# Edge attention with four gather buffers, two PSUM banks and the carried sums first; the message stage's first layer in pairs of steps

## What is computed

```python
# layer 0, for every edge
h = silu(edge_attr_8 @ fc_w1 / sqrt(8))                 # 8 -> 64: the first layer
w = (h @ fc_w2 / 8).reshape(-1, 5, 64)                  # 64 -> 320: the weights of five paths
# the weights times the sender's scalars and vectors make the messages, summed over each receiver

# layer 1, for every edge
scores = einsum(q[dst], k[src] + ef @ We + be) * scale * ew
m  = segment_max(scores, dst);  ex = exp(scores - m[dst])
out = segment_sum(ex / segment_sum(ex, dst)[dst] * v[src], dst)
# then the output projection, layer norms and a feed-forward of 1024
```

## Time and profile before

| What | us |
|---|---|
| median of three runs | 2969.75 |
| the profiled execution's own time | 2986.19 |
| its span | 2984.5 |
| message stage (164 steps) | about 70 to 1196 |
| order, projections, table of steps | about 1196 to 1476 |
| attention stage (96 steps) | about 1476 to 2777 |
| output stage | about 2777 to 2984 |

### The profile page before, as it was taken

The page is one execution under the profiler, slowest core; times in us unless marked ns, Lnnn a source line. Parts: engine busy times, 40 slices in busy tenths (PEclk is TensorE's granted clock), DMA queues, the critical chain, the costliest instruction groups (busy, mean ns, idle before and its releaser), DMA issues. The chain is left out here.

```text
span 2984.5 us, 40835 instructions
## 1 busy us (share of the span) xinstructions
PE 2102.1 (70%) x9125; PEld 1572.3 (53%) x9126; DVE 2219.6 (74%) x3394; ACT 1531.1 (51%) x4900; POOL 1741.0 (58%) x1849
## 2 busy tenths in 40 slices
PE   1699999999999999499235444455444554445898
PEld 0577777777777777233123333333333333333677
DVE  5688888888888888455367777777777787777555
ACT  0677777777777777133133333333333333333566
POOL 4477777777777777222266666666666666665011
PEclk8799999999999999699667777777777777777899
DMA  3422222222222222589566666666666666665000
GB/s 119 144 81 81 81 82 82 82 80 82 82 82 82 80 82 81 101 252 253 181 177 168 175 175 168 170 169 170 179 169 170 170 169 179 169 169 163 7 14 14
DMA packets 157682, 382.65 MB, mean 128 GB/s; under 512 B 47682, under 2 KB 62402, under 8 KB 157410
## 3 DMA queue, kind: packets, MB, share of 16 engines
q0 software_dynamic: 101968, 313.67, 37.6%
q1 hardware_dynamic: 55426, 57.40, 7.2%
q10 hardware_dynamic: 272, 11.42, 1.1%
HBM read 356.98 MB, written 36.80 MB: 132 GB/s over the span
## 5 line engine op out<-in xcount | busy, mean ns | idle before, releaser
L1497 PE MATMUL ps_sum<-kv_e,ident 128*128 128x264 f32 x1536 | 574.9, 552 | 693.0 <-issue 559.6
L1390 POOL DMA_INDIRECT kv_e<-kv_rows,edge x768 | 728.6, 949 | 430.1 <-issue 215.2
L413 POOL DMA_INDIRECT feat<-in_x_rows,idx x668 | 770.7, 1154 | 237.4 <-issue 236.0
L1497 PEld LDWEIGHTS ps_sum<-kv_e,ident 128*128 128x128 f32 x1536 | 427.0, 285 | 840.7 <-issue 696.4
L445 ACT ACTIVATE vsh<-feat,rec_a 128x256 f32<-128x256 f32 x1980 | 806.4, 495 | 24.9 <-DMA feat<-in_x_rows,idx 24.9
L1519 DVE TENSOR_TENSOR kv_e<-kv_e,ps_query 128x2048 f32<-128x2048 f32 x96 | 219.6, 2288 | 320.9 <-DMA kv_e<-kv_rows,edge 306.8
L489 PE MATMUL ps_a<-msg,hot 128*128 128x257 f32 x1312 | 409.2, 393 | 0.0
L491 PE MATMUL ps_a<-msg,hot 128*128 128x256 f32 x1312 | 390.3, 379 | 0.0
L1460 ACT ACTIVATE kept<-ps_sum,fade 128x33 f32<-128x33 f32 x768 | 147.2, 299 | 349.6 <-remote 349.6
L493 PE MATMUL ps_a<-msg,hot 128*128 128x192 f32 x1312 | 320.2, 325 | 0.0
L491 PEld LDWEIGHTS ps_a<-msg,hot 128*128 128x128 f32 x1312 | 248.5, 189 | 36.5
(11 more groups left out here) (344 smaller groups left out, 3031.5 us busy)
## 6 DMA issues: line engine op xcount, KB each, us to landing
ef<-in_ef_t SPq DMA_DIRECT2D x84, 256.0 KB
kv_e<-kv_rows,edge POOLq DMA_INDIRECT x768
rows_e<-in_ef_t ACTq DMA_DIRECT2D x1, 11152.0 KB, 39.3
rows_e<-rows SPq DMA_DIRECT2D x41, 272.0 KB
feat<-in_x_rows,idx POOLq DMA_INDIRECT x668
kv_rows<-kv SPq DMA_DIRECT2D x20, 260.0 KB
xw<-in_x_rows SPq DMA_DIRECT2D x22, 128.0 KB
emb<-in_emb_t SPq DMA_DIRECT2D x166, 16.0 KB
```

The lines of the kernel that those rows point to most:

```text
L413: pool.indirect_dma_start(out=feat[:, u, c, 0, :, :].rearrange("p a b -> p (a b)"), out_offset=None, in_=g.x_rows, in_offset=bass.Indirect ...
L1390: pool.indirect_dma_start(out=kv[:, u, s, :], out_offset=None, in_=g.kv_rows, in_offset=bass.IndirectOffsetOnAxis(ap=edge[:, u, s, DH + 1: ...
L1497: mm = pe.matmul(out, g.ident[:], kv[:, u, s, D:], start=(s == 0), stop=False, skip_group_check=True)
```

## The change

In the attention stage `kv`, the edge rows and the small tiles have four buffers instead of three (`RING = 4`), and POOL may be four steps ahead of PE; PSUM's sums and `kept` rotate over two (`BANKS = 2`). PE now waits for `v_kept` at the head of a step and makes the product of `kept` first; the eight slots follow. `v_sum` is gone: ACT waits for `v_used` of the former step instead. The number of steps stays 96 (24 laps of four for 32 of three). In the message stage the features of even steps lie on partitions 0 to 15 and those of odd steps on 64 to 79, with `g.w1` held in both places. Every second step PE makes the first layer of two steps, each product on 64 rows of the array, and it does so behind `weights`, no longer ahead of the wait for `m_prod`. Four loads of `fc_w1` take the place of two.

```diff
-RING = 3
+RING = 4
+BANKS = 2
@@ stage_tables
-                sp.dma_start(g.w1[half * NB:(half + 1) * NB, half * NH:(half + 1) * NH], g.fc_w1).then_inc(t_w, 16)
+                for step in range(2):
+                    at = step * NH + half * NB
+                    sp.dma_start(g.w1[at:at + NB, half * NH:(half + 1) * NH], g.fc_w1).then_inc(t_w, 16)
@@ stage_messages
-                sp.dma_start(emb[0:2 * NB, u % 2, :],
+                at = (u % 2) * NH
+                sp.dma_start(emb[at:at + 2 * NB, u // 2 % 2, :],
...
-            def hidden(u, landed):
-
-                pe.wait_ge(m_emb[u % 2], landed)
-                pe.matmul(ps_h[:, u % 2, 0:SUPER // 2], g.w1[:], emb[:, u % 2, :], start=True, stop=True,
-                          skip_group_check=True).then_inc(m_hps, 1)
+            def hidden_pair(u, landed):
+
+                pe.wait_ge(m_emb[0], landed)
+                pe.wait_ge(m_emb[1], landed)
+                for step in range(2):
+                    rows = slice(step * NH, (step + 1) * NH)
+                    pe.matmul(ps_h[:, step, 0:SUPER // 2], g.w1[rows, :], emb[rows, u // 2 % 2, :], start=True, stop=True,
+                              skip_group_check=True).then_inc(m_hps, 1)
...
-                    hidden(u, t * (16 * TURN // 2) + 16 * (u // 2 + 2))
                     pe.wait_ge(m_prod, i + 1 + TURN)
                     weights(i + 1, u + 1)
+                    if u % 2 == 0:
+                        hidden_pair(u + 2, t * (16 * TURN // 2) + 16 * (u // 2 + 2))
@@ stage_attend
-        kept = sb("kept", [P, RING, HEADS * HEAD])
-        ps_o = ctx.enter_context(nc.psum_tensor("ps_sum", [P, RING, 512], F32))
+        kept = sb("kept", [P, BANKS, HEADS * HEAD])
+        ps_o = ctx.enter_context(nc.psum_tensor("ps_sum", [P, BANKS, 512], F32))
...
-            pool.sem_inc(v_read, 2)
+            pool.sem_inc(v_read, RING - 1)
...
-                act.wait_ge(v_sum, k + 1)
+                act.wait_ge(v_used, k * 2 + 2 * RING)
                 act.sem_inc(g.asked, 1)
                 act.wait_ge(v_fade, k + 1)
                 for h in range(HEADS):
                     at_h = slice(h * HEAD, (h + 1) * HEAD)
-                    ins = act.activation(kept[:, u, at_h], ps_o[:, (u - 1) % RING, at_h], ACT.Copy,
+                    ins = act.activation(kept[:, u % BANKS, at_h], ps_o[:, (u - 1) % BANKS, at_h], ACT.Copy,
                                          scale=fade[:, u, h:h + 1])
...
-                    out = ps_o[:, u, 0:HEADS * HEAD]
+                    out = ps_o[:, u % BANKS, 0:HEADS * HEAD]
+                    pe.wait_ge(v_kept, k + 1)
+                    pe.matmul(out, g.ident[:], kept[:, u % BANKS, :], start=True, stop=False, skip_group_check=True)
                     for half in range(2):
                         pe.wait_ge(v_msg, k * 2 + half + 1)
                         for s in range(half * HALF, (half + 1) * HALF):
-                            mm = pe.matmul(out, g.ident[:], kv[:, u, s, D:], start=(s == 0), stop=False,
+                            mm = pe.matmul(out, g.ident[:], kv[:, u, s, D:], start=False, stop=(s == SLOTS - 1),
                                            skip_group_check=True)
                         mm.then_inc(v_used, 1)
-                    pe.wait_ge(v_kept, k + 1)
-                    pe.matmul(out, g.ident[:], kept[:, u, :], start=False, stop=True,
-                              skip_group_check=True).then_inc(v_sum, 1)
```

More of the change, by code:

```diff
@@ L331, in _ @@
                                          ALU.mult, ALU.mult)
-            dve.wait_ge(t_w, 16 * 2 * (1 + NPATH))
+            dve.wait_ge(t_w, 16 * 2 * (2 + NPATH))
             dve.tensor_scalar(g.w1[:], g.w1[:], 1.0 / float(np.sqrt(NB)), None, ALU.mult)
@@ L473, in weights @@
                     mm.then_inc(m_w, 1)
-            hidden(0, 16)
-            hidden(1, 16)
+            hidden_pair(0, 16)
             weights(0, 0)
@@ L1336, in stage_attend @@
         v_msg = ctx.enter_context(nc.semaphore("v_msg"))
-        v_sum = ctx.enter_context(nc.semaphore("v_sum"))
         v_acc = ctx.enter_context(nc.semaphore("v_acc"))
@@ L1402, in _ @@
             whole = act.value_load(g.laps_but_one[0:1, 0:1], min_val=1, max_val=MAX_LAPS)
-            act.sem_inc(v_sum, 1)
-            act.sem_inc(v_acc, 2)
+            act.sem_inc(v_acc, BANKS - 1)
             def point(i, u, w):
@@ L1436, in keep @@
                 w = window_of(act, i)
-                act.activation(g.acc[:, bass.ds(w, 1), :].rearrange("p a d -> p (a d)"), ps_o[:, u, 0:HEADS * HEAD],
+                act.activation(g.acc[:, bass.ds(w, 1), :].rearrange("p a d -> p (a d)"), ps_o[:, u % BANKS, 0:HEADS * HEAD],
                                ACT.Copy).then_inc(v_acc, 1)
-                act.wait_ge(v_acc, i + 3)
+                act.wait_ge(v_acc, i + BANKS)
                 act.sem_inc(g.asked, 1)
@@ L1465, in step @@
                     part((u + 2) % RING, (t + (u + 2) // RING) * 16 + 16)
-                keep(k, (u - 1) % RING)
+                keep(k, u - 1)
             act.wait_ge(v_const, 5)
@@ L1480, in _ @@
                 step(whole * RING + u, whole, u, u < RING - 2)
-            act.wait_ge(v_sum, whole * RING + RING + 1)
+            act.wait_ge(v_used, whole * (2 * RING) + 4 * RING)
             act.sem_inc(g.asked, 1)
```

## The result

The changed kernel takes 2952.98 us (median of 5 runs, 2950.25 to 2958.09), beside 2969.75 us for the kernel before in the same comparison: ratio 0.9948 [0.9937, 0.9959], 16.8 us faster. The forecast was 2761 us, with a range from 2740 to 2835. The profiled execution took 2952.27 us, with a span of 2950.5.

What follows compares the result with a forecast made beforehand. Attention was taken as bound by POOL's waits for a free buffer, messages by PE. Terms -188 (fourth buffer), -22 (pairs) and +1 (start) gave -209 us, from 2969.75 to 2761 us; range 2740 to 2835.

Steps and rivals of the forecast that it cites:

- What is left of the wait is 4.27 - 0.305 = 3.97 us every second step. The wait should go: Attention stage: a fourth buffer removes POOL's wait for PE, first to last gather 1082.2 us for 1270.2, -188.0 us.
- The product of `kept` first costs nothing: Attention stage: PE's `kept` product at the step's head is hidden by VectorE's keys; 59 us if that cover were gone.
- The first layer in pairs, -22: Message stage: paired products on different row halves shorten every second step; -22 us, bounds -35 and 0.
- The first product's earlier place: Message stage's very start: the pair no longer lies in PE's idle time, +1 us.
- the loads of `fc_w1`: Head of the kernel, SP's queue: two more loads taken as nothing, about 1 us if VectorE waited for them.
- two banks: Attention stage: the copy to `g.acc` must end before PE returns to the bank; queued behind `kept` on ACT, hidden.
- The saving is the same stalls in both: Whole kernel: profiled execution 16.4 us above the median, so -209 us was applied to 2969.75, giving 2761 instead of 2777.
- The late signal stays: Rival, attention: PE's signal stays some 8.7 us late every second step, now in the chain; +29 us, 2978; chance 0.08.
- The wait moves, the messages alone gain: Rival, attention: POOL fills the fourth buffer once, then waits as before, a step's chain taking 13.2 us; 2949; chance 0.08.
- The landings set the pace: Rival, attention: DMA queues make a step 12.0 us, so the gain is 119 us there; 2830; chance 0.08.
- a lateness from density alone: Attention: by the skill's rule, dense semaphore increments cause the lateness, no smaller in shorter steps; gives the late-signal rival's time.

Runs made afterwards that it cites:

- m3: Changed kernel in which POOL waits for ACT's word, passed on a step later, instead of PE's signal; 2773.24 us, no signal late.
- late job: Kernels timed together on one chip where traces show PE's signals late; the kernel before takes 2969.75 to 2982.99 us there.
- n2: Same kernel as m3, POOL waiting for ACT's word instead of PE's signal, in a late job; 2970.04 us beside 2974.18 for the whole change.
- q: Late job timing the unedited whole change, 2966.50 us, beside the kernel before with the message stage's pairs alone, 2955.05 us.
- prompt jobs: Jobs whose traces show PE's signals on time; the kernel before takes 2800.18 to 2803.13 us there.
- m2: Changed kernel with four buffers and two banks, but the product of `kept` last again with its own signal; 2772.61 to 2774.51 us over four such runs.
- q2: Kernel before with the message stage's pairs alone, attention stage unchanged, in a late job; 2955.05 us, 21.0 us under the kernel before.
- p1: Kernel before with the message stage's pairs alone, in a prompt job; this kernel is 20.5 and 23.9 us under the kernel before in such jobs.

## Why the prediction was wrong, step by step

**"What is left of the wait is 4.27 - 0.305 = 3.97 us every second step. The wait should go": -188.0, measured -17.6 from the first to the last gather, and -14.1 to PE's last product, between the two profiled executions.** The one of before stood 16.4 us above its median, so that by the medians (-16.8 in all, some -22 of it from the messages) attention gained nothing, and lost some 5 us. This is the step that failed. The arithmetic of POOL was right, as 1079.4 us in m3 for 1082.2 show, but a wait of POOL for a signal 8.7 us late was taken as a lack of buffers. In a late job the signals came out some 3.5 us after POOL had stopped in 46 of 47 late steps of before. With a further buffer POOL goes on longer, and the signals then come 11.0 to 11.5 us after the products for 8.4, 12.3 in n2: the wait that the buffer was to outlast grew with the buffer. A pair of steps stays at eighteen issues, 22.6 us, and a stand of about 4. The measured sums of the stands say so: 188 to 216 us in every kernel of a late job. What holds the signals is open.

**"The product of `kept` first costs nothing."** It was costed by the step in which the signal was on time. In the other kind of step the values' products queue behind a wait for ACT, which waits for the late signal, PE's clock falls meanwhile, and ACT's later work waits too: VectorE's keys, which waited for landings before, now wait for ACT's query part more than for landings. Groups by line, 1550 to 2650 us, of the changed kernel:

```profile
L1523 DVE TENSOR_TENSOR kv_e<-kv_e,ps_query 128x2048 f32<-128x2048 f32 x84 | 191.9, 2285 | 178.4 <-ACT ps_query L1431 126.0 <-issue 27.8 <-DMA kv_e<-kv_rows,edge 24.6
```

In q the attention part as a whole costs 11.5 us; which of its two edits does is open. In prompt jobs it costs nothing that can be seen, as forecast: m3, which has the new order, and m2, which has the old one, stand 0.6 us apart.

**The first layer in pairs, -22:** right. Steps of 6.67 and 6.39 (forecast 6.67 and 6.40), -20.5 to -23.9 us in three jobs. The Trainium skill, TensorEngine Tiling (Array Packing), section Performance Considerations, has the emptying of PSUM as what may take over as the bottleneck. The trace agrees: PE alone would have given 35 us, and about a third of it went into waiting for VectorE, which reads the products: its last messages end at 613.01 + 0.68 = 613.69, and the path weights start at 613.82.

**The first product's earlier place, the loads of `fc_w1`, two banks:** nothing of them is seen in the times.

**"The saving is the same stalls in both" (2777 turned into 2761).** The forecast against the profiled execution was 2777 us, and m3 takes 2773.24. That agreement says that the forecast describes a kernel without late signals, and it is in part luck, as the 2777 started from a level of 2986 and m3's from one of 2801. Where the 16 us taken off lay no run shows.

**The rivals.** "The late signal stays" named the mechanism and had 0.08. Its sum was wrong by its sizes: 27.1 us a pair where 26.1 were measured (1252.6/48). It took 6.74 us for each batch of values, a row of a stretch in which the granted clock was 0.50 (2003.28 to 2010.10). In the pair above one batch ran at 1.00 in 3.72 us and one mostly at 0.50 in 5.56, while the signal was not 8.7 but 12.4 us late. It ended at 2978, the kernel at 2953. The chance was too small by the prediction's own evidence: it could not name the cause of the lateness, and an unnamed delay on the only path between two engines can't be counted as gone. "The wait moves, the messages alone gain" gave 2949, nearest to 2953, and its sign is there, as POOL stands waiting 174.2 us for 202.5. But it says only that a step's chain takes 13.2 us anyhow, and not that this length hangs on a late signal: in m3, with the same work, a step takes 1079.4/96 = 11.2. "The landings set the pace" is out in prompt jobs: in m3 nine issues set it, at landings of 3.7 us.

From the warning of the Trainium skill on dense increments (VectorE: DVE Perf Modes, section on the TRN2 errata) the prediction took a lateness from density alone. The runs don't bear it out: m3 and n2 are one kernel with the same increments, and one has no late step, the other 47.

**Open.** What holds PE's signals in a late job, what makes a job late, and which edit costs the 11.5 us. Between q2 and p1, the same kernel, the gathers' duration (946 ns both) and the message stage are alike, with its DMA share (0.30 both) and VectorE's wait for PE's sums there (86.9 and 86.7 us). Apart from attention's pace and its waits, one row of the profile's page differs, that of the issues and their time to landing, of q2 and then of p1:

```profile
kv_e<-kv_rows,edge POOLq DMA_INDIRECT x768
```

```profile
kv_e<-kv_rows,edge POOLq DMA_INDIRECT x768, 3.7
```

No median stands in late jobs because most records of landings are missing: the trace of q2 holds 10,782, that of p1 31,624. So it is in all twenty traces, 10,782 to 16,273 in the six of late jobs and 31,560 to 31,729 in the fourteen of prompt ones, and records of engines' own signals are missing too (of `v_used` the changed kernel's trace holds 143 and m3's 194). The Trainium skill, NOTIFIC — the notification-queue block, section on overflow, says that a full record queue, depending on its mode, loses records or stalls the engine that produces them. That the recording itself delays PE's signals is the nearest rival left. Against it stands that records are missing in q2's message stage as well, where nothing is late; no run here tests it, as every execution on record has a granted clock and so was recorded.

## What to carry to other kernels

When a wait lasts longer than the work it waits for, find out what releases it before costing its removal. A further buffer outlasts a delay only if the delay stays as it is; here it grew from 8.4 to 11 us and more, and the chain that needs the signal each step (PE, ACT, PE) kept it. A wait for another engine's answer ahead of ready work is a risk while its signal is known to be late, though no run here parts its cost from the buffer's. Price a row with the clock at which it ran. And time the kernel before in several jobs: here its own level, 2801 or 2976 us, is ten times what the change is worth.

## What the runs showed of the hardware

- One kernel has two levels by job, 6% apart: medians of before 2800.18 to 2803.13 us in four jobs and 2969.75 to 2982.99 in three, and chip 10 showed both.
- On the upper level signals of PE arrive on average 8 to 12 us after the products in 47 to 49 of 95 steps, mostly some 3.5 us after POOL's last gather, whether POOL waits for PE (before) or for ACT (n2). Two that belong 1.78 us apart then come within 0.14 us in the changed kernel. In the message stage, where 668 gathers spread over some 1114 us, they are on time there.
- Products nobody needs raise the granted clock from 0.73 to 0.94 and leave the time alone where another engine sets the pace. Sixteen records of 264 columns take 3.72 us at 1.00, and 6.74 in a stretch nearly all at 0.50.
- Of the 0.30 us between two gathers of POOL 0.15 can be filled with other work: a memset of 0.12 us costs 0.01 us there, four that take 0.21 us lengthen the interval by 0.06.
